# A norm over whole batches: from a loop of eight passes to eight batches side by side, with the normalising on ScalarE

## What is computed

```
x = x + _L0_attn_b_ref(_layernorm(x, axis=-1), Wq, Wk, Wv)

def _L0_attn_b_ref(x, Wq, Wk, Wv):
    ...
    out = jnp.einsum('hbqk,hbkd->hbqd', atten, V).reshape(b, s, -1)
    y = out + x
    mu = jnp.mean(y, axis=(1, 2), keepdims=True)
    var = jnp.var(y, axis=(1, 2), keepdims=True)
    return (y - mu) / jnp.sqrt(var + EPS)
```

## Time and profile before

| what | us |
|---|---|
| median of three runs | 4397.89 |
| lowest and highest run | 4388.91, 4398.16 |
| the profiled execution, its own time | 4396.39 |
| its span from first to last instruction | 4394.7 |
| PE (TensorE) busy | 2982.2 (68%) |
| DVE (VectorE) busy | 2779.2 (63%) |
| POOL (GpSimd) busy | 2032.1 (46%) |
| ACT (ScalarE) busy | 1706.9 (39%) |
| mean granted TensorE clock | 0.809 of full speed |

### The profile page before, as it was taken

How to read it: one execution, slowest core, us unless ns; L and a number is a source line. 1 busy time by engine, 2 the same in 40 slices (tenths; PEclk the granted TensorE clock), 3 DMA queues, 4 the chain that set the end, 5 groups by cost and what they waited for, 6 DMA issues and landing times. The chain is left out here.

```text
span 4394.7 us, 67760 instructions
## 1 busy us (share of the span) xinstructions
PE 2982.2 (68%) x23775; PEld 1865.7 (42%) x23775; DVE 2779.2 (63%) x5980; ACT 1706.9 (39%) x3042; POOL 2032.1 (46%) x2610
## 2 busy tenths in 40 slices
PE   5848267775286477659588746688666888467856
PEld 3748111111286246548344334344243444244534
DVE  4634467874434762342488579677487886595678
ACT  2413246764122223334255512466422456124511
POOL 6653411100343303232355477355596464695686
PEclk9879579997598678879699867699777999576967
DMA  5122132210122002102222000222000221000000
GB/s 161 40 66 82 44 98 65 78 54 1 53 89 60 10 39 66 32 17 66 68 73 82 31 1 1 83 73 82 2 0 30 86 77 46 1 0 1 1 1 20
DMA packets 217167, 206.35 MB, mean 47 GB/s; under 512 B 49431, under 2 KB 194007, under 8 KB 216072
## 3 DMA queue, kind: packets, MB, share of 16 engines
q1 hardware_dynamic: 204552, 176.85, 12.5%
q0 software_dynamic: 12288, 25.19, 1.9%
HBM read 103.55 MB, written 96.47 MB: 46 GB/s over the span
## 5 line engine op out<-in xcount | busy, mean ns | idle before, releaser
L942 DVE TENSOR_REDUCE l0b_negm<-l0b_ps_s 128x2 f32<-128x1024 f32 x256 | 304.2, 1220 | 75.8 <-PE l0b_ps_s L713 75.1
L802 ACT ACTIVATE l0b_E<-l0b_ps_t 128x1024 f32<-128x1024 f32 x256 | 261.8, 1023 | 155.0 <-PE l0b_ps_t L695 154.5
L802 ACT ACTIVATE l2a_E<-l2a_ps_t 128x768 f32<-128x768 f32 (+1 forms) x192 | 169.1, 881 | 138.7 <-PE l2a_ps_t L695 138.5
L802 ACT ACTIVATE l3a_E<-l3a_ps_t 128x768 f32<-128x768 f32 (+1 forms) x192 | 169.1, 881 | 134.6 <-PE l3a_ps_t L695 134.4
L942 DVE TENSOR_REDUCE l2b_negm<-l2b_ps_s 128x2 f32<-128x256 f32 (+3 forms) x256 | 196.2, 818 | 31.4 <-PE l2b_ps_s L719 29.4
L802 ACT ACTIVATE l2b_E<-l2b_ps_t 128x768 f32<-128x768 f32 (+1 forms) x192 | 169.2, 881 | 119.7 <-PE l2b_ps_t L695 119.5
L942 DVE TENSOR_REDUCE l3a_negm<-l3a_ps_s 128x2 f32<-128x256 f32 (+3 forms) x256 | 196.2, 818 | 19.4 <-PE l3a_ps_s L719 16.6
L942 DVE TENSOR_REDUCE l2a_negm<-l2a_ps_s 128x2 f32<-128x256 f32 (+3 forms) x256 | 195.9, 817 | 17.1 <-PE l2a_ps_s L719 16.8
L883 POOL TENSOR_SCALAR_AFFINE_SELECT l2b_E<-l2b_E 128x256 f32<-128x256 f32 x256 | 101.0, 409 | 189.4 <-ACT l2b_E L802 189.2
L883 POOL TENSOR_SCALAR_AFFINE_SELECT l2a_E<-l2a_E 128x256 f32<-128x256 f32 x256 | 101.0, 407 | 173.5 <-ACT l2a_E L802 171.5
L883 POOL TENSOR_SCALAR_AFFINE_SELECT l3a_E<-l3a_E 128x256 f32<-128x256 f32 x256 | 101.0, 406 | 170.2 <-ACT l3a_E L802 168.3
(11 more groups left out here) (1013 smaller groups left out, 9357.2 us busy)
## 6 DMA issues: line engine op xcount, KB each, us to landing
room_up<-l0b_stack SPq DMA_DIRECT2D x32, 192.0 KB
room_down<-l0b_stack SPq DMA_DIRECT2D x32, 192.0 KB
room_up<-l2a_stack SPq DMA_DIRECT2D x32, 192.0 KB
room_down<-l2a_stack SPq DMA_DIRECT2D x32, 192.0 KB
room_up<-l2b_stack SPq DMA_DIRECT2D x32, 192.0 KB
room_down<-l2b_stack SPq DMA_DIRECT2D x32, 192.0 KB
room_up<-l3a_stack SPq DMA_DIRECT2D x32, 192.0 KB
room_down<-l3a_stack SPq DMA_DIRECT2D x32, 192.0 KB
```

The lines of the kernel that those rows point to most:

```text
L802: act.activation(probs(n % 3, c, 0)[:, 2 * p:2 * p + 2, :], ps_t[:, :, 0:width[c]], ACT.Exp, scale=scale).then_inc(probs_ready.sem, 1)
L942: e = dve.tensor_reduce(negm[:, qt, :, j], ps_s[n % 2][:, :, off:off + keys[qt]], AX.X, ALU.max, negate=True)
```

## The change

The stage is written without loops, and the eight batches' statistics lie side by side. VectorE takes all 32 bn_stats from XN directly, then all 8 aggregates; the small operations work on 8 columns at once, the matmul on 16 and the power on GpSimd on 8. The copies to xn, the memset of sq and the tiles xn and xs go. VectorE no longer normalises: it makes a shift of -mean x rstd, and ScalarE writes rstd x XN + shift back into XN, one ACTIVATE of 128x512 for each batch. VectorE adds each batch to X when its ACTIVATE is done.

```diff
--- before.py
+++ after.py
@@ -1107,64 +1107,72 @@
         def sb(n, shape, dt=FP32):
             return ctx.enter_context(nc.sbuf_tensor(f"{name}_{n}", shape, dt))
 
-        stats = sb("stats", [P, TB, 6])
-        mv = sb("mv", [P, 2])
-        both = sb("both", [P, 2])
-        sq = sb("sq", [P, 1])
-        mean = sb("mean", [P, 2])
-        msq = sb("msq", [P, 1])
-        var = sb("var", [P, 1])
-        rstd = sb("rstd", [P, 1])
+        stats = sb("stats", [P, B, TB, 6])
+        mv = sb("mv", [P, B, 2])
+        both = sb("both", [P, 2, B])
+        sq = sb("sq", [P, B])
+        mean = sb("mean", [P, 2, B])
+        msq = sb("msq", [P, B])
+        var = sb("var", [P, B])
+        rstd = sb("rstd", [P, B])
+        shift = sb("shift", [P, B])
         average = sb("average", [P, P])
-        xs = sb("xs", [P, TB, D])
-        xn = sb("xn", [P, TB, D])
-        ps = ctx.enter_context(nc.psum_tensor(f"{name}_ps", [P, 2], FP32))
-        sig = core.begin(dve_step=12, stats_ready=1, out_ready=1, sum_ready=1, rstd_ready=1)
-        dve_step, stats_ready, out_ready, sum_ready, rstd_ready = sig
+        ps = ctx.enter_context(nc.psum_tensor(f"{name}_ps", [P, 2, B], FP32))
+        sig = core.begin(dve_step=1, stats_ready=1, out_ready=1, sum_ready=1, rstd_ready=1, row_bias_ready=1, norm_ready=B)
+        dve_step, stats_ready, out_ready, sum_ready, rstd_ready, shift_ready, norm_ready = sig
         made = ctx.enter_context(nc.semaphore(f"{name}_made"))
         block = ctx.enter_context(nc.Block())
 
+        def batch(x, b):
+            return x[:, b * TB:(b + 1) * TB, :]
+
         @block.vector
         def _(dve):
+            ch = Chain(dve_step, dve, 0)
             dve.memset(average[:, :], 1.0 / P).then_inc(made, 1)
-            with dve.Fori(0, B) as i:
-                ch = Chain(dve_step, dve, i)
-                ch.link(dve.tensor_copy(xn[:, :, :], core.XN[:, bass.ds(i * TB, TB), :]))
+            for b in range(B):
                 for t in range(TB):
-                    e = dve.bn_stats(stats[:, t, :], xn[:, t, :])
-                ch.link(e)
-                dve.memset(sq[:, :], 0.0)
-                ch.link(dve.bn_aggr(mv[:, :], stats[:, :, :].rearrange("p t s -> p (t s)")))
-
-                dve.tensor_copy(both[:, 0:1], mv[:, 0:1])
-                ch.link(dve.tensor_tensor(sq[:, :], mv[:, 0:1], mv[:, 0:1], ALU.mult))
-                dve.tensor_tensor(both[:, 1:2], sq[:, :], mv[:, 1:2], ALU.add).then_inc(stats_ready.sem, 1)
-
-                dve.wait_ge(out_ready.sem, out_ready.at(i, 1))
-                ch.link(dve.tensor_copy(mean[:, :], ps[:, :]))
-                ch.link(dve.tensor_tensor(msq[:, :], mean[:, 0:1], mean[:, 0:1], ALU.mult))
-                ch.link(dve.tensor_tensor(var[:, :], mean[:, 1:2], msq[:, :], ALU.subtract))
-                dve.tensor_scalar(var[:, :], var[:, :], LN_EPS, None, ALU.add).then_inc(sum_ready.sem, 1)
-                dve.wait_ge(rstd_ready.sem, rstd_ready.at(i, 1))
-                ch.link(dve.tensor_scalar(xs[:, :, :], xn[:, :, :], mean[:, 0:1], rstd[:, 0:1], ALU.subtract, ALU.mult))
-                xi = core.X[:, bass.ds(i * TB, TB), :]
-                ch.link(dve.tensor_tensor(xi, xi, xs[:, :, :], ALU.add))
-                ch.close()
+                    e = dve.bn_stats(stats[:, b, t, :], core.XN[:, b * TB + t, :])
+            ch.link(e)
+            for b in range(B):
+                e = dve.bn_aggr(mv[:, b, :], stats[:, b, :, :].rearrange("p t s -> p (t s)"))
+            ch.link(e)
+            dve.tensor_copy(both[:, 0, :], mv[:, :, 0])
+            ch.link(dve.tensor_tensor(sq[:, :], mv[:, :, 0], mv[:, :, 0], ALU.mult))
+            dve.tensor_tensor(both[:, 1, :], sq[:, :], mv[:, :, 1], ALU.add).then_inc(stats_ready.sem, 1)
+            dve.wait_ge(out_ready.sem, out_ready.upto(1))
+            ch.link(dve.tensor_copy(mean[:, :, :], ps[:, :, :]))
+            ch.link(dve.tensor_tensor(msq[:, :], mean[:, 0, :], mean[:, 0, :], ALU.mult))
+            ch.link(dve.tensor_tensor(var[:, :], mean[:, 1, :], msq[:, :], ALU.subtract))
+            dve.tensor_scalar(var[:, :], var[:, :], LN_EPS, None, ALU.add).then_inc(sum_ready.sem, 1)
+            dve.wait_ge(rstd_ready.sem, rstd_ready.upto(1))
+            dve.scalar_tensor_tensor(shift[:, :], mean[:, 0, :], -1.0, rstd[:, :], ALU.mult, ALU.mult).then_inc(shift_ready.sem, 1)
+            for b in range(B):
+                dve.wait_ge(norm_ready.sem, norm_ready.upto(b + 1))
+                e = dve.tensor_tensor(batch(core.X, b), batch(core.X, b), batch(core.XN, b), ALU.add)
+            ch.link(e)
+            dve_step.per = ch.k
 
         @block.gpsimd
         def _(pool):
-            with pool.Fori(0, B) as i:
-                pool.wait_ge(sum_ready.sem, sum_ready.at(i, 1))
-                pool.tensor_tensor(rstd[:, :], var[:, :], core.minus_half[:, 0:1], ALU.pow).then_inc(rstd_ready.sem, 1)
+            pool.wait_ge(sum_ready.sem, sum_ready.upto(1))
+            pool.tensor_tensor(rstd[:, :], var[:, :], core.minus_half[:, 0:1].broadcast_to([P, B]), ALU.pow).then_inc(rstd_ready.sem, 1)
 
         @block.tensor
         def _(pe):
             pe.wait_ge(made, 1)
-            with pe.Fori(0, B) as i:
-                pe.wait_ge(stats_ready.sem, stats_ready.at(i, 1))
-                pe.matmul(ps[:, :], average[:, :], both[:, :], start=True, stop=True).then_inc(out_ready.sem, 1)
-
-    core.end(B, sig)
+            pe.wait_ge(stats_ready.sem, stats_ready.upto(1))
+            pe.matmul(ps[:, :, :].rearrange("p a b -> p (a b)"), average[:, :], both[:, :, :].rearrange("p a b -> p (a b)"),
+                      start=True, stop=True).then_inc(out_ready.sem, 1)
+
+        @block.scalar
+        def _(act):
+            act.wait_ge(shift_ready.sem, shift_ready.upto(1))
+            for b in range(B):
+                act.activation(batch(core.XN, b), batch(core.XN, b), ACT.Identity, bias=shift[:, b:b + 1],
+                               scale=rstd[:, b:b + 1]).then_inc(norm_ready.sem, 1)
+
+    core.end(1, sig)
 
 
 def single_head_attention_stage(core, name, w):
```

## The result

| | us |
|---|---|
| median of five runs, changed kernel | 4368.43 (4361.85 to 4369.80) |
| median of five runs, kernel before | 4397.89 (4385.44 to 4401.25) |
| ratio, with its 95% interval | 0.9939 (0.9921 to 0.9956) |
| the profiled execution of the changed kernel, its own time | 4369.80, span 4368.1 |

What follows compares the result with a forecast made beforehand. The norm stage, 49.1 us of chained passes alone between two boundaries, was taken to lie wholly on the program's path. Ten new terms summed to 18.6, 30.5 less, giving a forecast of 4366.5 us, range 4358 to 4371.

Steps and rivals of the forecast that it cites:

- the aggregates: Norm stage, VectorE: eight aggregates side by side at a pitch of 0.186 us, 1.59 us with the link.
- the small operations before the matmul: Norm stage: three small operations, run once on 8 columns instead of eight times on 1, 0.50 us.
- mean to epsilon: Norm stage, after the matmul: mean, msq, var and var plus epsilon, up to GpSimd's start, 0.84 us.
- the tail: End of the norm stage: eight ScalarE ACTIVATEs with VectorE's adds beside them, 6.47 us, bounds 5.9 to 10.9.
- ScalarE's form: Norm stage: ACTIVATE on 128x512 with scale and bias per partition, 0.802 us each, at a pitch of about 0.705.
- VectorE's tail: End of the norm stage if VectorE both normalised and added: 8 x (0.55 + 0.69) = 9.9 us or somewhat less.
- without overlap: Rival in the norm stage: ACTIVATEs don't overlap adds, up to 4.4 us, time 4370.9; likewise bn_stats and aggregates, 4369.6; 9%.
- TensorE's clock: Rival in the next stage: the granted clock rises later and gives the 30.5 us gain back; 1%.
- The boundary: Rival between last add and weight loads: 0.1 us more won, or a microsecond or so lost; 4365 to 4367.
- table load: Sign of a wrong forecast: a function table loaded on ScalarE ahead of the norm stage's first ACTIVATE.
- what is moved is the whole rest of the program: Everything behind the norm stage: it starts 30.5 us earlier, and no instruction moves within it.
- hardly more than 2 above by that: Whole program: by three runs' spread, the median could lie 6 us under the forecast but hardly 2 above.

Runs made afterwards that it cites:

- the ninth: Changed kernel with batch 0 normalised by VectorE and the bn_stats of batches 0 to 6 moved into the attention of layer 0: ratio 0.9915, median 4354.02 us.

## Why the prediction was right, and where it was not

**The working of the stage held, term by term.** Measured against forecast, in us: the memset 0.20 (0.19); the 32 bn_stats 6.31 (6.45), with a pitch of (6.28 - 0.277) / 31 = 0.194; the aggregates 1.16 (1.59); the small operations before the matmul 0.58 (0.50); the matmul 0.62 (0.65); mean to epsilon 0.86 (0.84); the power 1.68 (1.69); the shift 0.21 (0.21); the tail 6.47 (6.47). Sum 18.1 (18.6). The one term that was off by a good part is the aggregates': I built their pitch from the duration of one alone, 258 ns. Only the first of the row takes that; the tile's view of the changed kernel gives a median of 205, and the pitch is 0.13 where I had 0.186:

```profile
L1138 DVE BATCH_NORM_AGGREGATE l0b_out_mv<-l0b_out_stats x8: 204/205/262, 1092.9 to 1093.9; 128x2 f32<-128x24 f32 x8
```

**ScalarE's form, which no row of before had, came out as built up from three others:** 0.802 us was the estimate.

```profile
L1172 ACT ACTIVATE XN<-XN,l0b_out_shift,l0b_out_rstd x8: 798/799/812, 1098.0 to 1103.0; 128x512 f32<-128x512 f32 x8
```

Its pitch is (5.75 - 0.80) / 7 = 0.707, against 0.705. It sets the pace of the adds, as said: eight of them take 5.63, where in the version with VectorE alone they take 4.91. The Trainium skill, "ScalarE: Activation LUTs", section "Rules for kernel authors", gives add and mul to VectorE and not to ScalarE. The runs agree as to the single operation, 0.54 against 0.80; in the stage VectorE alone was 2.0 us slower. The forecast had VectorE's tail at 9.9 us "or somewhat less"; it is 8.7.

**The rivals.** No part ran without overlap. The prediction's price for that, a tail of 10.9, was also added up wrongly: 8 x 0.802 and then eight adds in 5.06 are 11.5, 5.0 over the 6.5 and not 4.4, which makes 4371.5, above the range that was to take this case in. TensorE's clock did not come back later in the next stage: it rose some 95 us behind the weight loads' issue, as before.

```profile
1198.00:1200.00 2.00, 2.00 (x12) 2.00 (x11) 0.00 (x0) 0.60 (x1) 0.96 (x1) 0.55 0.00 0
1200.00:1202.00 2.00, 2.00 (x20) 2.00 (x19) 0.57 (x1) 0.60 (x1) 0.96 (x1) 1.00 0.18 61
```

That is 1105.0 to about 1200, against 1130.5 to 1226. The boundary got shorter by 0.05 us with the loops gone, 0.50 from the last add to the first load against 0.55; 0.1 was allowed for. No table load stands ahead of the first ACTIVATE, and the stretch behind the stage is 1.1 us shorter, not longer.

**The step that failed is the one from the stage to the program's time**, and in it the size of one term, the wander of the whole from run to run. The prediction took all that isn't edited as fixed, "what is moved is the whole rest of the program", and bounded the measured time above by the spread of three runs, "hardly more than 2 above by that". The median of 4368.43 is 1.9 us above the forecast and inside the range that came of it, but the time by the ratio, 0.9939 x 4397.89 = 4371.1, is 4.6 above and just past the upper end of 4371.

What the runs showed in its place is a wander about three times as wide. Three runs had covered 4388.91 to 4398.16, 9 us; the kernel before went from 4385.44 to 4401.25 in five runs, from 4386.41 to 4402.15 in the twenty-three of the next set and from 4378.85 to 4405.94 in the seventeen of the last, 27 us. In the changed kernel's profile the attention ahead of the stage, which no edit touches, was 5.4 us longer, and it moved by 8.4 us between two profiles of the kernel before. TensorE's clock was looked at as a rival in the one stage behind the norm, and its changes went with the time in stages far from it. The range should have been some 5 us wider at the top.

On which side of 4371 the time fell was luck. The means of the same five and five runs are 4394.33 and 4367.38, 27 us apart, and the second lies well inside the range; the 4371.1 comes of setting the ratio on a median that is 3.6 above its mean. Timed once more, the ratio was 0.9927, on the other side of the 0.9929 to 0.9931 that 31.0 and 30.5 us give; both intervals hold it.

**How the 31.0 us divide:** 4.0 to the loop's turn (49.1 to 45.1), 25.0 to working on eight batches side by side with the copies gone (45.1 to 20.1), 2.0 to ScalarE beside VectorE (20.1 to 18.1), in this order of the steps. Most of the 25.0 is the chain of small operations with its two waits: from the first of them to the normalising it takes 1085.74 - 1083.25 = 2.49 us a pass, 19.9 for eight, and 1081.18 - 1077.43 = 3.75 once for all, 16.2 less. The eight copies are another 3.8 (1081.58 to 1082.05 in each pass, 0.47); the rest lies in the bn_stats, the aggregates, the normalising and the adds.

## What to carry to other kernels

What is taken out of a stage that stands alone between two barriers comes out of the program's time, here to within some 3 us, and a chain of short dependent steps repeated for each batch should be run once over all batches: the waits and small operations are then paid once, though a wait can grow (GpSimd's power went from 0.55 to 1.65 us for 8 columns, and eight times 0.55 was still more). An operation may go to an engine that is slower at it if it then lies beside the other's work. A change of under one per cent in a kernel whose untouched stages wander by several us each is read from the length of its own stage, and the total needs a range from the wander of the whole and not of three runs.

## What the runs showed of the hardware that was not expected

- One attention stage took 549.9 to 568.3 us over nine profiles, with the same code in eight of them and 28 instructions more in the ninth, at a granted clock of 0.87 to 0.81. The mixer took either 202.8 to 205.9 us, at 0.81 to 0.76, or 212.8 to 212.9, at 0.75 or 0.74.
- An aggregate over 24 numbers takes 258 ns alone and 205 behind another, at a pitch of (1.12 - 0.205) / 7 = 0.13 us. So in a row each instruction was shorter, and successive ones overlapped too.
- A hardware loop on VectorE, with the semaphores of a chained pass, cost 0.57 us a pass more than the same instructions written out: 0.6 from the second turn on (6.20 against 5.58) and half of that in the first.
